# Rows of the score operands ordered by part, dimension and copy, in a fused decoder layer

## The chip, the cores and the metric

One core of a Trainium2 chip runs one launch of a whole decoder layer. The metric is the device time of that launch in microseconds, median of 3 runs.

## What is computed

```python
x = layernorm(x + attn(x, U))                         # 4 of its lines, R = 32
x = layernorm(x + xattn(ctx, ctx, x, Wq, ..., bo))    # cross-attention
x = layernorm(x + ffn(x, ...))                        # fake-quantised gate, up, down

# xattn: x is (1, 1024, 128), ctx is (1, 6404, 128), 16 heads of depth 8
qh = split_heads(q @ Wq + bq)
kh = split_heads(k @ Wk + bk)
vh = split_heads(v @ Wv + bv)
logits = einsum('bhsd,bhtd->bhst', qh, kh) / sqrt(8)
out = einsum('bhst,bhtd->bhsd', softmax(logits), vh)
return out @ Wo + bo
```

The cross-attention is nearly all of the work: 1024 queries against 6404 context rows in 16 heads.

## The kernel before

**Stages.** The first stretch, to about 118 us, does the first attention block and projects the context: for each of 17 chunks of 384 context rows (CK = 384, the last one partly filled) the keys are made in float32 and split into three bf16 parts, whose sum is the float32 key. They are written to an array in the chip's main memory, `k_parts_dram` [chunk, part, 128, CK]; the projected queries go the same way to `q_parts_dram` [half, part, 128, 512]. The middle stretch computes scores, exponentials and values. The last one, from about 820 us, projects the output, normalises and does the feed-forward block.

**Phases.** The middle stretch has 8 phases: 4 groups of 4 heads by 2 halves of 512 queries. Each phase goes over the 17 key chunks. For every chunk TensorE computes scores (line 1282: bf16, 59 rows contracted, 32 keys by 512 queries each) into PSUM, ScalarE turns most of them into exponentials (line 708, 128 x 1536 at a time, 67 instructions in a phase), VectorE computes the others with a polynomial (lines 958 to 984), and TensorE multiplies the result with the values (line 1312).

**The score operands.** A head has 8 dimensions (DH). A product of two float32 numbers is made of seven products of their bf16 parts, so that a head needs 7 x 8 = 56 contraction rows; three more rows carry a shift (59 = KR). `k_op` and `q_op` hold these rows on the partitions: two heads (i) lie side by side in a row, and the other two heads of the group (r, R2 = 2) lie 64 partitions on (W2 = 64). One row of `k_op` is 2 x 384 bf16 numbers, 1536 bytes; a row of `q_op` is 2048 bytes.

**The loads.** `load_k` (line 279) fills one of 4 slots (KS) of `k_op` for one chunk and group. It issues six DMAs at line 290: for each r one of 24 rows (key parts 0, 1, 2) and two of 16 rows (key parts 0 and 1, twice). `load_q` (line 295) fills one of 2 slots of `q_op` for one phase: for each r three DMAs at line 306, of 24, 16 and 16 rows, each of one query part read 3 or 2 times by a step of zero, and one of three rows for the shift (line 310). A slot has its own semaphore, and a DMA adds 16 to it: K_LOAD = 96 for a `load_k`, Q_LOAD = 128 for a `load_q`.

**Who issues them.** All these DMAs are issued by SyncE (SP in the profile, its queue SPq), one after the other in program order. In a phase it runs 12 `load_k` in a loop on the device (line 485, three turns of four; the address in main memory is worked out in registers by `sp.snap`), then one `load_k` for the last chunk, then `load_q` for the next phase, then four `load_k` for the next phase's first four chunks with fixed addresses, then, from the second phase on, four small DMAs of results at line 503 (`o_t<-att_rows`, 8 rows each). A `load_k` of slot s waits until TensorE has done the scores of the chunk that held s before (`scores_done`), four chunks back.

**Who waits for them.** TensorE waits for the next chunk's slot after the third block of scores of the present chunk, and for `q_loaded` at the start of a phase:

```python
if s == 2 and m + 1 < PHASES * NC:
    wait(k_loaded[(m + 1) % KS], at(K_LOAD * ((m + 1) // KS + 1), K_LOAD // KS))
```

Ahead of the first phase SyncE also issues the load for chunk 0 (line 420), the first `load_q` (448), the loads of chunks 1 to 3 (452), and only behind these the stores of the last four key chunks (454), for all of which it then waits before the loop of the first phase. A path for large scores (`general_shift_...`) calls the same two functions; it is not taken with these inputs.

Of the kernel before, what the change touches and what calls it, by code (L numbers as in the profile page):

```python
# [29 lines left out]
P = 128  # L30
# [4 lines left out]
HQ = 512  # L35
# [5 lines left out]
CK = CT * P  # L41
H = 16
DH = D // H
G = 4
NG = H // G
R2 = 2
G2 = G // R2
KR = 59
W2 = P // R2
# [40 lines left out]
def decoder_layer(nc, x, ctx_in, U, Wq, bq, Wk, bk, Wv, bv, Wo, bo, clip_x, clip_down,  # L90
                  w_gate, w_up, w_down, out, score_limit=SCORE_LIMIT):
    stack = ExitStack()
    with stack:
        def sb(name, shape, dt=F32):
            return stack.enter_context(nc.sbuf_tensor(name, shape, dt))
# [70 lines left out]
        k_op = sb("k_op", [P, KS, G2, CK], BF16)  # L166
        q_op = sb("q_op", [P, 2, G2, HQ], BF16)
# [111 lines left out]
        def load_k(sp, slot, chunk, group, signal, counter=None, count=None):  # L279


            src = k_parts_dram[chunk, 0, group, :]
            rows = P // (NG * R2)
            starts = [sp.snap(src.offset + r * (rows * CK)) for r in range(R2)]
            if counter is not None:

                sp.wait_ge(counter, count)
            for r in range(R2):
                for a, b, parts in ((0, 24, 3), (24, 40, 2), (40, 56, 2)):
                    sp.dma_start(k_op[W2 * r + a:W2 * r + b, slot, :, :].rearrange("p i t -> p (i t)"),  # L290
                                 bass.AP(src.tensor, starts[r],
                                         [[P * CK, parts], [G2 * CK, DH], [1, G2 * CK]])
                                 ).then_inc(signal, 16)

        def load_q(sp, slot, half, group_rows, group, signal, counter=None, count=None):

            src = q_parts_dram[half, 0, group_rows, :]
            rows = P // (NG * R2)
            starts = [[sp.snap(src.offset + n * (P * HQ) + r * (rows * HQ)) for r in range(R2)]
                      for n in range(3)]  # L300
            if counter is not None:

                sp.wait_ge(counter, count)
            for r in range(R2):
                for n, (a, b, copies) in enumerate(((0, 24, 3), (24, 40, 2), (40, 56, 2))):
                    sp.dma_start(q_op[W2 * r + a:W2 * r + b, slot, :, :].rearrange("p i t -> p (i t)"),  # L306
                                 bass.AP(src.tensor, starts[n][r],
                                         [[0, copies], [G2 * HQ, DH], [1, G2 * HQ]])
                                 ).then_inc(signal, 16)
                sp.dma_start(q_op[W2 * r + 56:W2 * r + 59, slot, :, :].rearrange("p i t -> p (i t)"),  # L310
                             shift_dram[half, group, :, G2 * r:G2 * r + G2, :].rearrange("j i t -> j (i t)")
                             ).then_inc(signal, 16)


        def general_shift_sp(sp):

            with sp.Fori(0, 2) as half:
                with sp.Fori(0, NG) as g:
                    n = half * NG + g
                    load_q(sp, 0, half, bass.ds(g * 32, 32), g, g_q_loaded, g_turned, n + 1)  # L320
                    with sp.Fori(0, NC) as c:
                        load_k(sp, 1, c, bass.ds(g * 32, 32), g_k_loaded,
                               g_scores_done, n * (NC * G) + c * G + 1)
                    dst = shift_dram[half, g, 0, :, :]
                    offsets = [sp.snap(dst.offset + j * (G * HQ)) for j in range(3)]
                    sp.wait_ge(g_shift_step, 5 * n + 5)
                    for j in range(3):
                        sp.dma_start(bass.AP(dst.tensor, offsets[j], [[P, 4], [HQ, G], [1, P]]),
                                     shift_parts[:, j, :]).then_inc(shift_written, 16)
# [51 lines left out]
        def _(sp):  # L381
# [36 lines left out]

            sp.wait_ge(k_parts_written[0], 16)
            load_k(sp, 0, 0, slice(0, 32), k_loaded[0])  # L420

            with sp.Fori(2, NC // 4) as r:
# [23 lines left out]
            sp.wait_ge(zero_shift_written, 16)  # L446
            sp.wait_ge(q_parts_written, 32)
            load_q(sp, 0, 0, slice(0, 32), 0, q_loaded[0])

            sp.wait_ge(scores_done, AHEAD)  # L450
            for c in range(1, KS):
                load_k(sp, c, c, slice(0, 32), k_loaded[c], k_parts_written[c], 16)
# [9 lines left out]
            with sp.If(sp.value_load(flag[0:1, 0:1]) > 0):  # L462
                all_written()
                sp.wait_ge(k_loaded[1], K_LOAD)
                general_shift_sp(sp)
                sp.wait_ge(shift_written, 48 * 2 * NG)

                load_q(sp, 0, 0, slice(0, 32), 0, g_q_loaded, g_turned, 2 * NG + 1)

                load_k(sp, 1, 1, slice(0, 32), g_k_loaded, g_scores_done, 2 * NG * NC * G + 1)  # L470
# [1041 lines left out]
```

## Time and profile before

| what | value |
|---|---|
| median of 3 runs | 873.7 us (872.42 to 881.33) |
| the profiled execution, its own time | 870.89 us |
| its span | 869.2 us |
| busy: PE, DVE, ACT, POOL | 719.9, 689.8, 738.2, 169.0 us |
| mean granted clock of TensorE | 0.953 of full speed |
| bytes read and written in main memory | 30.15 and 6.42 MB |

The span is what the profiler saw between the first and the last instruction; the execution's own time has 1.7 us more around it. PE is TensorE, DVE VectorE, ACT ScalarE, POOL GpSimd. SyncE computes nothing, so that the busy table of the page has no row for it; its DMA-issuing instructions stand in the views as SPq with a duration of their own, which is the time the issuing takes, not the transfer.

### The profile page before, as it was taken

The page shows a single profiled execution, that of the slowest core. Times are in us where ns is not written, and L with a number is a line of the kernel's source. Part 1 is how long each engine was busy: PE and PEld are TensorE (multiplying, and loading weights), DVE is VectorE, ACT ScalarE, POOL GpSimd, SP SyncE. Part 2 cuts the span into 40 slices and gives each one's busy share as a digit, 9 for nine tenths or more (in the row PEclk, how much of TensorE's full clock was granted, in tenths as well). Part 3 has the DMA queues.
Part 4 walks back from the last instruction along what each step waited for, and adds up shares of the span by engine and source line. Part 5 has one row for each costly group of instructions (what it writes and reads, how often), then busy time and mean ns, then how long its engine had stood idle before and what let it go on. Part 6 is the DMA issues. An engine that isn't in the chain of part 4 may idle for free.

```text
span 869.2 us, 38041 instructions
## 1 busy us (share of the span) xinstructions
PE 719.9 (83%) x15210; PEld 321.5 (37%) x15212; DVE 689.8 (79%) x1952; ACT 738.2 (85%) x650; POOL 169.0 (19%) x304
## 2 busy tenths in 40 slices
PE   6987678878899889879997899699878998899851
PEld 3435334423443344324433343233323443344331
DVE  3428749975999699939995999589958996899866
ACT  2446779997999999969997999799979997999842
POOL 2502412211222122202220222112211221122100
PEclk9999789998999999989999999999999999999965
DMA  3213321111111111111111111111111111111000
GB/s 104 77 55 115 126 82 35 33 42 40 36 34 40 40 36 36 40 39 37 35 38 41 36 35 36 44 36 35 35 44 37 35 35 44 37 34 35 23 1 25
DMA packets 31714, 38.38 MB, mean 44 GB/s; under 512 B 3534, under 2 KB 30192, under 8 KB 31616
## 3 DMA queue, kind: packets, MB, share of 16 engines
q1 hardware_dynamic: 30748, 36.57, 13.9%
q8 instruction: 65, 1.06, 0.5%
q10 hardware_dynamic: 868, 0.48, 0.2%
q14 instruction: 33, 0.27, 0.1%
HBM read 30.15 MB, written 6.42 MB: 42 GB/s over the span
## 4 chain that ended last, share of the span: by engine, by line
SPq 28%; ACT 25%; issue 18%; PE 17%; DMA 6%; DVE 5%; POOL 1%; ACTq 1%; POOLq 0%; DVEq 0%
SPq L290 24%; ACT probs L708 23%; PE ps L1312 7%; DMA k_op<-k_parts_dram 4%; PE ps L1282 3%; SPq L306 2%; PE ps L1211 2%; PE ps L1197 2%; SPq L503 1%; DMA k_parts_dram<-k_parts 1%; DVE stats L774 0%; POOL k_parts L539 0%; PE ps L1160 0%; DMA q_parts_dram<-q_parts 0%; DVE probs L1091 0%
## 5 line engine op out<-in xcount | busy, mean ns | idle before, releaser
L708 ACT ACTIVATE probs<-ps 128x1536 f32<-128x1536 f32 (+1 forms) x536 | 673.9, 1372 | 48.4 <-PE ps L1282 47.3
L1312 PE MATMUL ps<-probs,v_op 64*9 64x512 f32 (+1 forms) x8384 | 528.0, 503 | 48.2 <-DMA k_op<-k_parts_dram 42.2
L1282 PE MATMUL ps<-q_op,k_op 59*32 59x512 bf16 x6432 | 344.0, 386 | 52.0 <-ACT probs L708 42.5
L977 DVE SCALAR_TENSOR_TENSOR e_u<-e_u,e_f 128x256 f32<-128x256 f32 x720 | 259.6, 426 | 0.0
L1282 PEld LDWEIGHTS ps<-q_op,k_op 59*32 59x32 bf16 x6432 | 114.9, 91 | 318.7 <-issue 240.8
L1312 PEld LDWEIGHTS ps<-probs,v_op 64*9 64x9 f32 x8384 | 166.0, 87 | 139.0 <-issue 50.7
L958 DVE TENSOR_SCALAR e_t<-ps 128x256 f32<-128x256 f32 x240 | 90.7, 419 | 105.2 <-PE ps L1282 96.8
L586 POOL TENSOR_SCALAR e_pow<-e_t 128x512 int32<-128x512 int16 x120 | 74.3, 619 | 364.7 <-DVE e_t L958 364.7
L579 POOL COPY v_op<-v_all 128x108 f32<-128x108 f32 x136 | 62.6, 460 | 215.0 <-PE ps L1312 214.3
L977 DVE SCALAR_TENSOR_TENSOR e_u<-e_f 128x256 f32<-128x256 f32 x240 | 90.1, 417 | 0.2
L984 DVE SCALAR_TENSOR_TENSOR probs<-e_u,e_pow 128x256 f32<-128x256 f32 x240 | 89.6, 411 | 0.0
L964 DVE SCALAR_TENSOR_TENSOR e_f<-ps,e_t 128x256 f32<-128x256 f32 x240 | 89.4, 414 | 0.0
L539 POOL TENSOR_TENSOR k_parts<-probs,k_parts 128x384 bf16<-128x384 f32 x17 | 17.5, 1034 | 65.5 <-ACT k_parts L638 65.5
L665 ACT ACTIVATE probs<-ps,neg_n 128x1024 f32<-128x1024 f32 x8 | 8.9, 1115 | 16.8 <-PE ps L1211 16.8
L1160 PE MATMUL ps<-ctx_t,wk_turned 128*128 128x384 f32 x34 | 15.8, 547 | 6.4 <-ACT ctx_t L617 3.4
L625 ACT ACTIVATE kf<-ps,bias_cols 128x384 f32<-128x384 f32 x17 | 9.8, 579 | 8.8 <-PE ps L1160 8.8
L1163 PEld LDWEIGHTS ps<-wv_sb,ctx_t 128*128 128x128 f32 x102 | 14.8, 200 | 4.9 <-issue 0.6
L1211 PE MATMUL ps<-y_rhs,y_lhs 64*128 64x512 f32 x32 | 15.6, 611 | 0.7 <-DVE v_all L809 0.7
L1197 PE MATMUL ps<-probs,x_nat 128*128 128x512 f32 x32 | 15.6, 615 | 0.0
L638 ACT ACTIVATE k_parts<-probs 128x384 bf16<-128x384 f32 x17 | 8.8, 520 | 7.8 <-DVE probs L824 7.8
L809 DVE TENSOR_TENSOR v_all<-ps,bv_bc 128x384 f32<-128x384 f32 (+1 forms) x17 | 9.4, 556 | 7.5 <-PE ps L1163 7.4
L1163 PE MATMUL ps<-wv_sb,ctx_t 128*128 128x128 f32 x102 | 14.8, 283 | 0.0
(177 smaller groups left out, 247.1 us busy)
## 6 DMA issues: line engine op xcount, KB each, us to landing
k_op<-k_parts_dram SPq DMA_DIRECT2D x544, 24.0 KB
k_op<-k_parts_dram SPq DMA_DIRECT2D x272, 36.0 KB
k_parts_dram<-k_parts SPq DMA_DIRECT2D x17, 288.0 KB, 2.8
ctx_nat<-in_ctx_dram SPq DMA_DIRECT2D x16, 192.0 KB, 2.6
q_op<-q_parts_dram SPq DMA_DIRECT2D x32, 32.0 KB
q_parts_dram<-q_parts SPq DMA_DIRECT2D x2, 384.0 KB, 3.8
q_op<-q_parts_dram SPq DMA_DIRECT2D x16, 48.0 KB
x_nat<-in_x_dram SPq DMA_DIRECT2D x1, 512.0 KB, 3.7
```

The costliest lines, as they stand in the source:

```text
L290: sp.dma_start(k_op[W2 * r + a:W2 * r + b, slot, :, :].rearrange("p i t -> p (i t)"), bass.AP(src.tensor, starts[r], [[P * CK, parts], [G2 ...
L579: pool.tensor_copy(v_op[:, slot].rearrange("p j (h d) -> p j h d", h=G), v_all[:, bass.ds(tile, CT), head:head + G, :]).then_inc(v_staged, 1)
L586: pool.tensor_scalar(e_pow[:], e_low(e_t[:]), float(2 ** 23), float(EXP2_LEAD), ALU.mult, ALU.add).then_inc(e_pow_ready, 1)
L708: act.activation(probs[:, b % NP].rearrange("p u t -> p (u t)")[:, 0:columns], ps[:, bank:bank + BU, :].rearrange("p u t -> p (u t)")[:, 0 ...
L958: dve.tensor_scalar(e_t[:, cols], score, E_MIN, ROUND, ALU.max, ALU.add).then_inc(e_step, 1)
L964: dve.scalar_tensor_tensor(out=e_f[:, cols], in0=score, scalar=E_MIN, in1=e_low(e_t[:, cols]), op0=ALU.max, op1=ALU.subtract).then_inc(e_s ...
L977: dve.scalar_tensor_tensor(out=e_u[:, cols], in0=u[:, cols], scalar=a, in1=e_f[:, cols], op0=ALU.add, op1=ALU.mult).then_inc(e_step, 1)
L984: dve.scalar_tensor_tensor(out=probs[:, block % NP, BU - 1, 512 - EW + cols.start:512 - EW + cols.stop], in0=e_u[:, cols], scalar=EXP2[0], ...
L1197: last = pe.matmul(ps[:, 4 + b, :], x_nat[:, j, :], attn_e[:, j, HQ * b:HQ * b + HQ], start=(j == 0), stop=(j == TQ - 1), skip_group_check ...
L1211: last = pe.matmul(ps[:, 2 * (j % 2) + b, :], y_lhs[:, P * j:P * j + P], y_rhs[:, HQ * b:HQ * b + HQ], start=True, stop=True)
L1282: return pe.matmul(ps[a:a + P // G, bank, :], k_op[W2 * r:W2 * r + KR, kslot, i, P * j + a:P * j + a + P // G], q_op[W2 * r:W2 * r + KR, q ...
L1312: last = pe.matmul(ps[32 * k:32 * k + DH + 1, ACC[h], a:b], v_op[W2 * h:W2 * h + W2, slot, j, (DH + 1) * k:(DH + 1) * (k + 1)], probs[W2 * ...
```

## The change

Both operands keep seven blocks of 8 rows, and the seven pairs of parts are the same; their order changes. Before, a DMA's rows were ordered by part or copy first and dimension second (24, 16, 16 rows). Now they are grouped by the part of the key: rows 0 to 23 are key part 0 in three copies against the three query parts, rows 24 to 47 are key part 1 in the same way, rows 48 to 55 are key part 2 against query part 0. Within a DMA the dimension is the leading index, with 8 values, and the copy or part comes second. `load_k` now reads with a step of zero, and `load_q` reads several parts. The number of DMAs is the same (six and eight), as are the rows and bytes. `load_k` makes six start addresses where it made two; `load_q` makes two where it made six.

```diff
@@ load_k
-            starts = [sp.snap(src.offset + r * (rows * CK)) for r in range(R2)]
+            starts = [[sp.snap(src.offset + n * (P * CK) + r * (rows * CK)) for r in range(R2)]
+                      for n in range(3)]
...
             for r in range(R2):
-                for a, b, parts in ((0, 24, 3), (24, 40, 2), (40, 56, 2)):
-                    sp.dma_start(k_op[W2 * r + a:W2 * r + b, slot, :, :].rearrange("p i t -> p (i t)"),
-                                 bass.AP(src.tensor, starts[r],
-                                         [[P * CK, parts], [G2 * CK, DH], [1, G2 * CK]])
+                for part, (a, copies) in enumerate(((0, 3), (24, 3), (48, 1))):
+                    sp.dma_start(k_op[W2 * r + a:W2 * r + a + DH * copies, slot, :, :
+                                      ].rearrange("p i t -> p (i t)"),
+                                 bass.AP(src.tensor, starts[part][r],
+                                         [[G2 * CK, DH], [0, copies], [1, G2 * CK]])
                                  ).then_inc(signal, 16)
@@ load_q
-            starts = [[sp.snap(src.offset + n * (P * HQ) + r * (rows * HQ)) for r in range(R2)]
-                      for n in range(3)]
+            starts = [sp.snap(src.offset + r * (rows * HQ)) for r in range(R2)]
...
             for r in range(R2):
-                for n, (a, b, copies) in enumerate(((0, 24, 3), (24, 40, 2), (40, 56, 2))):
-                    sp.dma_start(q_op[W2 * r + a:W2 * r + b, slot, :, :].rearrange("p i t -> p (i t)"),
-                                 bass.AP(src.tensor, starts[n][r],
-                                         [[0, copies], [G2 * HQ, DH], [1, G2 * HQ]])
+                for a, parts in ((0, 3), (24, 3), (48, 1)):
+                    sp.dma_start(q_op[W2 * r + a:W2 * r + a + DH * parts, slot, :, :
+                                      ].rearrange("p i t -> p (i t)"),
+                                 bass.AP(src.tensor, starts[r],
+                                         [[G2 * HQ, DH], [P * HQ, parts], [1, G2 * HQ]])
                                  ).then_inc(signal, 16)
```

On SyncE, one `load_k` in the loop of the first phase was the following. ISA is the register instruction that works out an address; 24x1x768 and 16x1x768 are DMAs of 24 and 16 rows.

```order
L290 ISA
L290 DMA k_op<-k_parts_dram 24x1x768
L290 DMA k_op<-k_parts_dram 16x1x768 x2
L290 ISA
L290 DMA k_op<-k_parts_dram 24x1x768
L290 DMA k_op<-k_parts_dram 16x1x768 x2
```

The same `load_k` in the changed kernel (its line 291):

```order
L291 ISA
L291 DMA k_op<-k_parts_dram 24x1x768
L291 ISA
L291 DMA k_op<-k_parts_dram 24x1x768
L291 ISA
L291 DMA k_op<-k_parts_dram 8x768
L291 ISA
L291 DMA k_op<-k_parts_dram 24x1x768
L291 ISA
L291 DMA k_op<-k_parts_dram 24x1x768
L291 ISA
L291 DMA k_op<-k_parts_dram 8x768
```

Two DMAs of 24 rows and four of 16 became four of 24 and two of 8, and four more register instructions stand between them. Nothing else moved on SyncE in the loop.

Between two phases SyncE issues a `load_q` and four `load_k` with fixed addresses. Their start was:

```order
L306 DMA q_op<-q_parts_dram 24x1x1024
L306 DMA q_op<-q_parts_dram 16x1x1024 x2
L310 DMA q_op<-shift_dram 3x1024
L306 DMA q_op<-q_parts_dram 24x1x1024
L306 DMA q_op<-q_parts_dram 16x1x1024 x2
L310 DMA q_op<-shift_dram 3x1024
L290 DMA k_op<-k_parts_dram 24x1x768
L290 DMA k_op<-k_parts_dram 16x1x768 x2
```

and is now:

```order
L307 DMA q_op<-q_parts_dram 24x1x1024 x2
L307 DMA q_op<-q_parts_dram 8x1024
L312 DMA q_op<-shift_dram 3x1024
L307 DMA q_op<-q_parts_dram 24x1x1024 x2
L307 DMA q_op<-q_parts_dram 8x1024
L312 DMA q_op<-shift_dram 3x1024
L291 DMA k_op<-k_parts_dram 24x1x768 x2
L291 DMA k_op<-k_parts_dram 8x768
```

The sizes changed in the same way, with no register instructions in either.

## Rows read from the trace of the kernel before

**Rows 1.** Timeline, SyncE: start us, us, line, operation, count in a row.
```profile
383.70 2.70 SPq L503 DMA_DIRECT2D o_t<-att_rows  x4
386.80 64.30 SPq L290 DMA_DIRECT2D k_op<-k_parts_dram  x78
451.14 2.05 SPq L306 DMA_DIRECT2D q_op<-q_parts_dram  x3
453.23 0.44 SPq L310 DMA_DIRECT2D q_op<-shift_dram  x1
453.71 2.07 SPq L306 DMA_DIRECT2D q_op<-q_parts_dram  x3
455.82 0.44 SPq L310 DMA_DIRECT2D q_op<-shift_dram  x1
456.30 17.07 SPq L290 DMA_DIRECT2D k_op<-k_parts_dram  x24
```

**Rows 2.** Waits of SyncE, whole span: us in total, times, longest us.
```profile
SPq L290 <- PE ps L1282: 8.7, 16, 0.8
```

**Rows 3.** Timeline, ScalarE, around a change of phase.
```profile
429.25 32.49 ACT L708 ACTIVATE probs<-ps 128x1536 f32<-128x1536 f32 x26
465.13 1.45 ACT L708 ACTIVATE probs<-ps 128x1536 f32<-128x1536 f32 x1 [3.39 <-PE ps L1282]
```

**Rows 4.** Waits from 118 to 820 us.
```profile
ACT probs L708 <- PE ps L1282: 44.3, 25, 5.7
PE ps L1312 <- DMA k_op<-k_parts_dram: 42.2, 34, 4.9
```

**Rows 5.** Timeline around the last load.
```profile
810.41 11.60 ACT L708 ACTIVATE probs<-ps 128x1024 f32<-128x1024 f32 x9
810.47 2.04 SPq L290 DMA_DIRECT2D k_op<-k_parts_dram  x3
```

**Rows 6.** Line 290, whole span: duration ns min/median/max, first and last start us.
```profile
L290 SPq DMA_DIRECT2D k_op<-k_parts_dram x816: 611/658/834, 36.8 to 811.9; - x164
L290 SPq FUSED_REGOPS  x192: 42/47/80, 117.9 to 805.6; - x192
```

**Rows 7.** Line 290, single instructions: of 24 rows, of 16 rows, address.
```profile
L290 SPq DMA_DIRECT2D k_op<-k_parts_dram x1: 741/741/741, 424.3 to 424.3; - x1
L290 SPq DMA_DIRECT2D k_op<-k_parts_dram x1: 630/630/630, 425.9 to 425.9; - x1
L290 SPq MOVE k_op<-k_parts_dram x1: 38/38/38, 425.1 to 425.1; - x1
```

**Rows 8.** DMAs by size: count, KB each (page, part 6).
```profile
k_op<-k_parts_dram SPq DMA_DIRECT2D x544, 24.0 KB
k_op<-k_parts_dram SPq DMA_DIRECT2D x272, 36.0 KB
q_op<-q_parts_dram SPq DMA_DIRECT2D x32, 32.0 KB
q_op<-q_parts_dram SPq DMA_DIRECT2D x16, 48.0 KB
```

**Rows 9.** DMA packets and queues, from 376 to 465 us.
```profile
DMA packets 2336, 3.36 MB, mean 38 GB/s; under 512 B 288, under 2 KB 2176, under 8 KB 2326
q1 hardware_dynamic: 2326, 3.21, 12.1%
```

**Rows 10.** Other DMAs that SyncE issues: duration ns min/median/max.
```profile
L385 SPq DMA_DIRECT2D ctx_nat<-in_ctx_dram x16: 328/342/432, 1.3 to 83.8; - x16
L310 SPq DMA_DIRECT2D q_op<-shift_dram x16: 417/437/440, 95.1 to 727.1; - x16
L503 SPq DMA_DIRECT2D o_t<-att_rows x28: 624/637/687, 294.0 to 814.6; - x28
L435 SPq DMA_DIRECT2D ctx_nat<-in_ctx_dram x1: 662/662/662, 86.9 to 86.9; - x1
L414 SPq DMA_DIRECT2D shift_dram<-zeros_bf x1: 894/894/894, 35.9 to 35.9; - x1
```

**Rows 11.** Engines busy from 118 to 812 us, granted clock, DMA share.
```profile
118.00:812.00 694.00, 599.91 (x14302) 258.21 (x14291) 588.32 (x1680) 648.65 (x518) 132.94 (x248) 0.98 0.13 37
```

## The prediction

> **What bounds the kernel now.** The busy table offers ScalarE, so I began with the stretch of the eight phases: of 694 us ScalarE is busy 649, TensorE 600 at 0.98 of full clock, and the DMA engines only 0.13 [rows 11]. Bandwidth is free; ScalarE is near the bound, but not on it. The second view was what ScalarE waits for: 44.3 us in 25 waits for scores, and TensorE in turn 42.2 us for the key load [rows 4]. At a change of phase ScalarE runs without a pause and then stands 3.39 us [rows 3]. The third view says why the load is late: SyncE's timeline has no hole. 78 DMAs in 64.30 us, then 5.1 us of query DMAs, then 24 DMAs in 17.07 us [rows 1]. Its waits for freed slots, of which there could be over a hundred, come to 8.7 us in all [rows 2]. The turns of a phase add to 2.70 + 0.4 + 64.30 + 5.2 + 17.07 = 90 us, from 383.70 to 473.4. So what sets the length of a phase is the time that SyncE takes to issue, and ScalarE comes only 6 us behind (44.3 over seven changes of phase). The last `load_k` ends at 812.5, and the last exponentials at 822.0 [rows 5]: nine of them, about 1.3 us each, of which the last three belong to the last chunk. The last chunk's scores begin at about 817. A load lands 2 to 3 us after its issue (an estimate: the first of the 17.07 us run was issued by 460.6, and ScalarE goes on at 465.13 [rows 3], behind some 2 us of values and scores). So there are no more than 2 us to spare at the end.
>
> Hence a microsecond added to SyncE between 93 and 812 us costs one; one taken away gains one until about 44 are gone.
>
> **What the change does to that.** There are 136 `load_k` and 8 `load_q` [rows 8]; the first `load_k` lies in the setup, where it costs nothing. On SyncE's path that is 135 x 2 + 16 = 286 DMAs of 24 rows and 135 x 4 + 32 = 572 of 16 rows. A DMA of 24 rows takes 0.74 us to issue, one of 16 rows 0.63 to 0.66, I take 0.64 [rows 7]; the median of all is 0.658 [rows 6]. Before: 286 x 0.74 + 572 x 0.64 = 578 us. After: 572 of 24 rows at an unknown price, and 286 of 8 rows.
>
> The 8-row DMA has a near relative: line 503 moves 8 rows of 2048 bytes with the 8 leading, 0.637 us [rows 10]. 286 x 0.64 = 183 us. Below it could go to 0.44 (three rows, line 310), above to 0.69 (the longest of line 503): minus 57 to plus 15 us.
>
> The 24-row DMA whose leading count is 8 stands nowhere. First, what the leading count does. From 376 to 465 us SyncE issues 115 DMAs, and there are 288 packets under 512 bytes, though no row is that short [rows 9]: about 2.5 end marks for each DMA. Key loads led by 3, 2 and 2 would give 7 for three DMAs, 2.33 each, and the 8-row ones of line 503 more. A DMA thus runs on as many engines as its leading count lets it, and with 8 it runs on 8. Second, what issuing costs by that count: for rows without a second index 3 engines cost 0.437 and 8 cost 0.637 (lines 310 and 503), 0.04 for each engine more; 16 cost only 0.342 (line 385), so it isn't the number of rows (there 128). For rows with a second index 2 cost 0.63, 3 cost 0.74 [rows 7], 4 cost 0.662 (line 435, 128 rows), 8 cost 0.894 (line 414, 96 rows, a first issue behind a wait). From 2, 3 and 4 engines with 0.04 for each more one comes to 0.87, 0.94 and 0.82; line 414 says 0.89. I take 0.87. Lower end: 0.437, if what counts is rows per engine, which fall from 8 to 3; upper end: 1.27, if the step from 2 to 3 (0.107) goes on for six engines. 572 x 0.87 = 498 us. So the DMAs cost 498 + 183 - 578 = +103 us.
>
> The address instructions: `load_k` in the loop has 6 where it had 2. One takes 47 ns [rows 6]. To it comes a gap: of the 0.82 us per DMA in the loop (64.30 over 78) 0.66 are the DMA, 0.04 its MOVE [rows 7] and 0.02 its share of the old address instructions, which leaves 0.10 for some 2.3 gaps, 0.045 each. 96 loads x 4 x 0.09 = +35 us; from 18 (no gap) to 40. (SPq's 192 of them are these two for each of the 96 loads [rows 6].) Outside the loop addresses are fixed and nothing is added, and `load_q`'s four fewer don't exist at run time.
>
> The transfers get shorter: a DMA's engine moved 8 rows, now 3 or 1. A packet takes about 74 ns (12.1% of 16 x 89 us over 2326 packets) [rows 9], and an engine's are in series, so the last one lands some 0.4 us earlier. As SyncE sets the rate, that shifts the pipeline once: -0.4 us. TensorE's matmuls, 59 rows, are unchanged.
>
> Sum: +103 + 35 - 0.4, less up to 2 us spare at the end: +136. Against the profiled execution's own 870.9 us (2.8 below the median, near the fastest run): 1007 us. A loop load then takes SyncE 5.0 + 0.7 + 0.4 = 6.1 us, and ScalarE has work for 4.9 (32.49 us for 26, four to a chunk): it stands in every chunk, where it stood only at phase starts. That cover is what the kernel loses.
>
> Two rules of the Trainium skill bear on this. The trace has the end marks above. DMA: Bandwidth & Descriptors, Why a DMA increments its semaphore by 16 and not by 1, states that the engine count is the largest number up to 16 that divides both patterns' slowest dimension: 3, 2, 2 before and 8, 8, 8 now; the trace agrees in its 2.5 marks. The same page, Issuing engines are not separate DMA queues, calls the sequencer's time to initiate a DMA "usually small relative to the DMA itself". By that the change could only help. This trace disagrees: 0.66 us of issuing stands against 8 packets of 74 ns.
>
> **The rivals.**
> - **The price stays where 24 rows are now**, 0.74, whatever the leading count. For: the same 24 rows. Against: line 503 beside line 310. 572 x 0.74 = 423, + 183 - 578 = +28, with the addresses and less the 2 us +61: 932 us.
> - **All shapes with an 8 in front cost as line 503**, 0.64, since the second index costs nothing there. For: 4 engines with 128 rows cost 0.662. Against: line 414. 366 + 183 - 578 = -29, +35: 875 us, within 1%.
> - **Issuing gets cheaper with rows per engine.** At 0.55 for 24 rows and 0.5 for 8: 315 + 143 - 578 = -120, +35. SyncE then leaves the path and ScalarE takes it; the gain ends at its 44 us of waiting, from 827 to 860 us, say 845. Against: 16 and 24 rows both have 8 rows per engine and differ by 0.11; line 503 has one row per engine and costs 0.637.
> - **The landing decides, not the issuing**: TensorE waits for transfers on 2 or 3 engines, and 8 shorten each of the eight waits by 0.4 us: 868 us. For: rows 4 name the DMA. Against: no hole in rows 1, and the addresses would still count.
> - **Each engine costs 0.107 in these shapes**, so 1.27: +229 more, 1236 us. For: the step from 16 to 24 rows. Against: lines 435 and 414. TensorE falling to the lower clock as it waits more would also land above my range.
>
> **How the numbers follow.** A measurement of this kernel can tell about 1% from no change. Forecast 0.57 (973 to 1047 by prices of 0.81 to 0.94); price stays 0.17; as line 503 0.08; cheaper 0.07; landing 0.04; 1.27 or another slowdown above 0.07. Slower by over 1% takes the first, the second and the last, and a third of the line 503 case: 0.83. Within 1%: 0.08. Faster by over 1%: 0.09. The range: upward 1055, downward through the case at 932 and nearly to the one at 875, 880; what is left out is 0.07 above and some 0.15 below.
>
> **What would show it.** In the profile of the changed kernel: line 291's 24-row DMAs at 0.87 us and the 8-row ones at 0.64; 576 FUSED_REGOPS instead of 192; 8 end marks per DMA, so about 850 packets under 512 B per phase; SyncE without holes, phases of some 107 us; ScalarE waiting for scores 150 us or more, in over 100 waits; TensorE waiting for `k_op` in most chunks. Wrong would be: 24-row DMAs at or below 0.65, holes in SyncE's timeline, or a phase under 92 us.

## The result, and the profile after

The changed kernel takes 833.5 us, median of 4 runs, against 873.4 us before in the same comparison: ratio 0.955, 95% interval 0.948 to 0.961. It is faster by 40 us where I had forecast 136 us slower. The profiled execution took 833.0 us, its span 831.3.

The timeline of SyncE in the changed kernel, the counterpart of [rows 1]. The query loads are now line 307 and 312, the key loads line 291, the result copies line 505:

```profile
366.66 2.73 SPq L505 DMA_DIRECT2D o_t<-att_rows  x4
369.78 61.32 SPq L291 DMA_DIRECT2D k_op<-k_parts_dram  x78
431.14 1.91 SPq L307 DMA_DIRECT2D q_op<-q_parts_dram  x3
433.09 0.27 SPq L312 DMA_DIRECT2D q_op<-shift_dram  x1
433.41 1.91 SPq L307 DMA_DIRECT2D q_op<-q_parts_dram  x3
435.36 0.29 SPq L312 DMA_DIRECT2D q_op<-shift_dram  x1
435.69 15.56 SPq L291 DMA_DIRECT2D k_op<-k_parts_dram  x24
```

There is still no hole, but a round of this list, from 366.66 to 451.3, is 84.6 us where it was 90. Every piece that holds loads is shorter: 61.32 us for 64.30, 15.56 for 17.07 (16.7 to 16.9 in the other phases before). Line 312 is of special interest, since the change doesn't touch it: 0.27 and 0.29 us for 0.44.

Its waits: SyncE's (as [rows 2]), then from 118 to 820 us ScalarE's and TensorE's (as [rows 4]):

```profile
SPq L291 <- PE ps L1284: 8.4, 17, 0.7
...
ACT probs L710 <- PE ps L1284: 10.1, 17, 4.2
PE ps L1314 <- DMA k_op<-k_parts_dram: 9.1, 8, 4.0
```

ScalarE's timeline over the same change of phase as the first fence (as [rows 3]):

```profile
353.92 11.86 ACT L710 ACTIVATE probs<-ps 128x1536 f32<-128x1536 f32 x9
365.97 83.71 ACT L710 ACTIVATE probs<-ps 128x1536 f32<-128x1536 f32 x67 [0.20 <-PE ps L1284]
```

ScalarE does the 67 exponentials of a phase in 83.71 us without a pause. Its wait at the seven changes of phase was 1.4 to 5.7 us; here it is 0.2, and nowhere over 0.5. Of its 44.3 us of waiting 10.1 are left, 4.2 of them in one wait inside the first phase.

TensorE's clock tells the same story. Before, TensorE stood at a change of phase until a key load landed, and the clock granted to it then fell to its lower level, 1.2 GHz. The first row is TensorE's timeline before, the second the stretch that follows it, the third the changed kernel from 129 to 794 us (of the two stretches: start:end and length in us, the busy us of PE, PEld, DVE, ACT and POOL, then the granted clock):

```profile
463.10 1.16 PE L1312 MATMUL ps<-probs,v_op 64*9 64x512 f32 x16 [3.30 <-DMA k_op<-k_parts_dram]
463.96:467.37 3.41, 3.41 (x56) 2.09 (x48) 0.00 (x0) 1.52 (x2) 0.28 (x1) 0.50 0.13 41
129.00:794.00 665.00, 595.61 (x14443) 259.62 (x14429) 593.21 (x1696) 651.44 (x522) 139.13 (x248) 1.00 0.13 39
```

The trace of before shows such a fall at six of the seven changes of phase, for 3.4 or 6.8 us each; the changed kernel has none in that stretch. No run isolates what these falls cost. They come behind a late load, and the account of SyncE's time below needs nothing from them.

Line 291 over the whole span (as [rows 6]), and then single DMAs of it (as [rows 7]): 24 rows and 8 rows inside the loop, 24 rows and 8 rows among those with fixed addresses, and last the unchanged DMA of three rows, all 16 of them:

```profile
L291 SPq DMA_DIRECT2D k_op<-k_parts_dram x816: 278/685/1377, 36.9 to 771.7; - x164
L291 SPq FUSED_REGOPS  x576: 37/37/85, 117.2 to 767.5; - x192
...
L291 SPq DMA_DIRECT2D k_op<-k_parts_dram x1: 685/685/685, 402.1 to 402.1; - x1
L291 SPq DMA_DIRECT2D k_op<-k_parts_dram x1: 311/311/311, 403.0 to 403.0; - x1
L291 SPq DMA_DIRECT2D k_op<-k_parts_dram x1: 664/664/664, 448.1 to 448.1; - x1
L291 SPq DMA_DIRECT2D k_op<-k_parts_dram x1: 461/461/461, 448.8 to 448.8; - x1
L312 SPq DMA_DIRECT2D q_op<-shift_dram x16: 257/272/287, 95.6 to 691.7; - x16
```

The 576 address instructions are there as foreseen. The prices are not: 24 rows cost 0.66 to 0.70 us and not 0.87, 8 rows 0.31 or 0.46 and not 0.64.

Packets of one phase, 359 to 443 us, against [rows 9]:

```profile
DMA packets 2935, 3.35 MB, mean 40 GB/s; under 512 B 894, under 2 KB 2774, under 8 KB 2924
```

The small packets went from 288 to 894 in a phase, and 102 key DMAs with 8 end marks each make 816 of them. Read as the prediction reads them, one mark for each engine, each key DMA does run on 8 engines. That part of the change does what its shape says, and it isn't where the time came from, as the experiments show.

### The profile page after: what moved, and what is told of

It reads as the page before. It is cut to its first block, busy times and chain, and to the rows that moved or that the text cites. A ratio compares the mean times of both kernels' runs of the same rounds, so it can differ in the third digit from the quotient of the medians.

```text
span 831.3 us, 38425 instructions
## 1 busy us (share of the span) xinstructions
PE 707.7 (85%) x15210; PEld 319.9 (38%) x15212; DVE 689.5 (83%) x1952; ACT 736.0 (89%) x650; POOL 174.9 (21%) x304
## 4 chain that ended last, share of the span: by engine, by line
ACT 40%; issue 24%; PE 16%; SPq 10%; DVE 5%; DMA 3%; POOL 1%; ACTq 1%; POOLq 0%; DVEq 0%
ACT probs L710 39%; SPq L291 8%; PE ps L1314 6%; PE ps L1284 3%; PE ps L1213 2%; PE ps L1199 2%; DMA k_op<-k_parts_dram 2%; SPq L505 1%; DMA k_parts_dram<-k_parts 1%; PE ps L1162 1%; DVE stats L776 1%; PE ps L1449 1%; ACTq L723 1%; POOL k_parts L541 0%; DMA q_parts_dram<-q_parts 0%
## 5 line engine op out<-in xcount | busy, mean ns | idle before, releaser
L1284 PE MATMUL ps<-q_op,k_op 59*32 59x512 bf16 x6432 | 337.4, 382 | 60.7 <-ACT probs L710 56.4
L1284 PEld LDWEIGHTS ps<-q_op,k_op 59*32 59x32 bf16 x6432 | 107.9, 90 | 331.5 <-issue 245.7
L1314 PEld LDWEIGHTS ps<-probs,v_op 64*9 64x9 f32 x8384 | 169.3, 86 | 90.2 <-issue 27.7
L581 POOL COPY v_op<-v_all 128x108 f32<-128x108 f32 x136 | 68.3, 502 | 181.3 <-PE ps L1314 180.6
L1009 DVE STREAM_TRANSPOSE att_rows<-acc_t 128x512 f32<-128x512 f32 x7 | 5.0, 711 | 15.6 <-DMA o_t<-att_rows 15.6
L1165 PEld LDWEIGHTS ps<-wv_sb,ctx_t 128*128 128x128 f32 x102 | 15.5, 208 | 5.2 <-issue 1.2
```

Of the source, the lines that this page charges most:

```text
L581: pool.tensor_copy(v_op[:, slot].rearrange("p j (h d) -> p j h d", h=G), v_all[:, bass.ds(tile, CT), head:head + G, :]).then_inc(v_staged, 1)
L1284: return pe.matmul(ps[a:a + P // G, bank, :], k_op[W2 * r:W2 * r + KR, kslot, i, P * j + a:P * j + a + P // G], q_op[W2 * r:W2 * r + KR, q ...
L1314: last = pe.matmul(ps[32 * k:32 * k + DH + 1, ACC[h], a:b], v_op[W2 * h:W2 * h + W2, slot, j, (DH + 1) * k:(DH + 1) * (k + 1)], probs[W2 * ...
```

## The experiments

My theory after the result (A) was that the time of the eight phases is still SyncE's issuing time, one for one, and that I had the prices wrong. The rival (B) was that the 8 engines bring the rows in sooner, and the issuing follows from that.

### The dimension in front, and nothing else (lead_only)

```diff
-                                         [[P * CK, parts], [G2 * CK, DH], [1, G2 * CK]])
+                                         [[G2 * CK, DH], [P * CK, parts], [1, G2 * CK]])
...
-                                         [[0, copies], [G2 * HQ, DH], [1, G2 * HQ]])
+                                         [[G2 * HQ, DH], [0, copies], [1, G2 * HQ]])
```

> The kernel before with its row groups of 24, 16 and 16, its two addresses per load_k and its six DMAs; only the dimension (8) is put in front within each DMA. Theory A (issuing sets the time; what fell is mostly the price of the small DMA, which isn't here): 24 rows at 0.66 to 0.70 us, 16 rows at 0.60 to 0.64, a load_k cheaper by 0.1 to 0.3 us, 840 to 860 us. Theory B (the engine count is what matters, by landing or by issuing, and row sizes don't): 835 us or less, as after or better, since it has no added addresses.

Measured: 883.75 us, ratio to before 1.016 (1.013 to 1.019). It is slower by 1.6%, little but clear of the noise. The range of A was missed by 24 us, and B by 49: with 8 engines in every load the kernel is slower than with 2 and 3. Two DMAs of its loop, of 16 and of 24 rows:

```profile
L290 SPq DMA_DIRECT2D k_op<-k_parts_dram x1: 685/685/685, 410.5 to 410.5; - x1
L290 SPq DMA_DIRECT2D k_op<-k_parts_dram x1: 689/689/689, 411.4 to 411.4; - x1
```

24 rows became cheaper (0.74 to 0.69), but 16 rows dearer (0.63 to 0.66 before), and there are twice as many of them. That is what my range had wrong: I had put 16 rows led by 8 at 0.60 to 0.64.

### The new row groups, with the part or copy in front (sizes_only)

```diff
-                                         [[G2 * CK, DH], [0, copies], [1, G2 * CK]])
+                                         [[0, copies], [G2 * CK, DH], [1, G2 * CK]])
...
-                                         [[G2 * HQ, DH], [P * HQ, parts], [1, G2 * HQ]])
+                                         [[P * HQ, parts], [G2 * HQ, DH], [1, G2 * HQ]])
```

(against the changed kernel)

> The changed kernel with its row groups of 24, 24 and 8 and its six addresses, but the copy or part (3) put back in front of the dimension in the 24-row DMAs. Theory A: 24 rows at 0.72 to 0.74 us, 8 rows at 0.31 in the loop and 0.46 outside, together 0.1 to 0.2 us less per load_k than before: 845 to 860 us. Theory B: most of the load runs on 3 engines as before and the addresses cost, so 871 us or more.

Measured: 848.6 us, ratio 0.977 (0.972 to 0.983), as A expected. More than half of the gain is there with the 24-row DMAs still led by 3, and with the added addresses paid. It comes from the 8-row DMA that takes the place of a 16-row one: all of these together average 0.345 us, and the 16-row ones before averaged 0.640. A 24-row DMA in its loop:

```profile
L291 SPq DMA_DIRECT2D k_op<-k_parts_dram x1: 722/722/722, 412.6 to 412.6; - x1
```

### Four more addresses, or rather two (addresses)

```diff
-            starts = [sp.snap(src.offset + r * (rows * CK)) for r in range(R2)]
+            starts = [[sp.snap(src.offset + n * (P * CK) + r * (rows * CK)) for r in range(R2)]
+                      for n in (0, 1, 1)]
...
-                                 bass.AP(src.tensor, starts[r],
+                                 bass.AP(src.tensor, starts[n][r],
```

> The kernel before with six start addresses per load_k instead of two, DMAs of the same shapes (the two 16-row DMAs read key parts 1 and 2 in place of 0 and 1, so that part of each score product is another one; the work is the same). If the added register instructions cost what they last and their gaps (0.083 us each, 384 of them) on the queue that sets the time: 871 + 32 = 903 us. If they are hidden behind the issuing of the DMA before them: within 4 us of 871, with the durations of the DMAs shorter by what the registers take.

Measured: 888.8 us, ratio 1.020 (1.018 to 1.022). The compiled kernel merged the second and the third address, which are the same number, so that 192 were added and not the 384 that the expectation counts:

```profile
L291 SPq FUSED_REGOPS  x384: 37/37/85, 119.8 to 826.0; - x192
...
395.87 67.22 SPq L291 DMA_DIRECT2D k_op<-k_parts_dram  x78
```

17.3 us for 192 is 0.090 us each: nothing is hidden. It is the price that the prediction used. 78 DMAs with 24 added addresses take 67.22 us for 64.30 in [rows 1]. That pair differs by more than most; over the seven phases whose loop stands by itself in the timeline the mean went from 65.0 to 67.2 us, which is 0.090 for each address again. The DMAs' own durations are unchanged. (The kernel's result is another one, since it reads other parts; only its time is used.)

### The price of one shape by itself (probe)

SyncE issues four DMAs of one shape in a row, waits until they have landed, and goes on to the next, such as:

```diff
+            for i in range(4):
+                sem(sp.dma_start(dst[0:8, i, 0:384], a([[384, 8], [1, 384]])))
+            settle()
...
+            for i in range(4):
+                sem(sp.dma_start(dst[0:24, i, 0:384], a([[384, 8], [49152, 3], [1, 384]])))
+            settle()
```

> No decoder layer at all: SyncE alone issues four DMAs of one shape in a row, waits until all have landed, then the next shape; the output is zeros. Theory P1 (my prediction's: price grows with the engines, 0.04 us each, plus something for a second index): simple 3, 8 rows at 0.44, 0.64; 8x3 at 0.8 or more. Theory P2 (price grows with rows and index, not engines; a small DMA is short, and waits at its start for the rest of the one before it): simple 8 rows at 0.28 to 0.32 when the one before is small, 0.46 behind 8x3; 3 rows 0.27 behind 8 rows and 0.44 behind 2x8; 8x3 at 0.66 to 0.70. Source in SBUF: 0.62 if it is the source that makes line 503's dear, 0.3 if not.

Issue durations, ns min/median/max. In this order: simple 8 rows of 1536 bytes, 8 of 2048, 3 rows, 16 rows; then with a second index (the leading count first) 3x8, 2x8, 8x3, 8x2, 8x3 with a step of zero, 4x6, 16x3, 8x7; last 8 rows from SBUF:

```profile
L44 SPq DMA_DIRECT2D dst<-in_ctx_dram x4: 277/295/395, 2.2 to 3.3; - x4
L50 SPq DMA_DIRECT2D dst<-in_ctx_dram x4: 272/295/297, 7.3 to 8.3; - x4
L56 SPq DMA_DIRECT2D dst<-in_ctx_dram x4: 240/272/274, 12.3 to 13.2; - x4
L62 SPq DMA_DIRECT2D dst<-in_ctx_dram x4: 316/418/422, 17.0 to 18.3; - x4
L71 SPq DMA_DIRECT2D dst<-in_ctx_dram x4: 689/706/800, 28.8 to 31.1; - x4
L74 SPq DMA_DIRECT2D dst<-in_ctx_dram x4: 614/620/638, 33.9 to 35.9; - x4
L77 SPq DMA_DIRECT2D dst<-in_ctx_dram x4: 662/668/686, 38.5 to 40.6; - x4
L80 SPq DMA_DIRECT2D dst<-in_ctx_dram x4: 663/666/670, 42.8 to 45.0; - x4
L83 SPq DMA_DIRECT2D dst<-in_ctx_dram x4: 662/664/667, 47.2 to 49.3; - x4
L86 SPq DMA_DIRECT2D dst<-in_ctx_dram x4: 623/623/634, 51.5 to 53.5; - x4
L89 SPq DMA_DIRECT2D dst<-in_ctx_dram x4: 592/592/620, 55.9 to 57.8; - x4
L95 SPq DMA_DIRECT2D dst<-in_ctx_dram x4: 662/672/693, 65.6 to 67.8; - x4
...
L68 SPq DMA_DIRECT2D dst<-src_sb x4: 624/638/778, 24.6 to 26.8; - x4
```

A second index costs about as much as all the rest: 0.27 to 0.42 us for simple patterns, 0.59 to 0.71 with one. With 8 in front, rows and bytes don't matter in it: 16, 24 and 56 rows (8x2, 8x3, 8x7) have minima of 0.663, 0.662 and 0.662. Reading through a step of zero costs the same as reading apart. The rows also repeat what the loop showed: from 3x8 to 8x3 the 24 rows get cheaper, from 2x8 to 8x2 the 16 rows get dearer.

The same kernel then issues DMAs in mixed order. An 8-row one right behind two of 24 rows (8x3), a 3-row one behind 16 rows (2x8), a 3-row one behind 8 simple rows:

```profile
L105 SPq DMA_DIRECT2D dst<-in_ctx_dram x2: 461/464/467, 78.5 to 80.5; - x2
L109 SPq DMA_DIRECT2D dst<-in_ctx_dram x2: 426/428/429, 82.9 to 84.1; - x2
L117 SPq DMA_DIRECT2D dst<-in_ctx_dram x2: 272/272/273, 90.0 to 90.6; - x2
```

A small DMA right behind one with a second index takes some 0.16 us more than by itself. So part of such a DMA's cost is booked on its successor. That is the second half of P2: line 310's 0.437 in [rows 10] was 0.27 of its own and 0.16 of the 16-row DMA ahead of it. It also fits that an 8-row load costs 0.31 in the loop and 0.46 outside: in the loop an address instruction and a MOVE stand between, and they seem to take that time in its place. No run varies this alone.

### Rows from SBUF (probe_source)

The same, with other shapes, such as `sp.dma_start(dst[0:3, i, :], src_sb[32:35, :])`.

> SyncE's issuing by itself again, output zeros. My prediction took line 503 (8 rows, source in SBUF, 0.637) for the price of 8 rows from main memory. Theory S (the source in SBUF makes a DMA dear whatever its rows): 0.5 to 0.65 for 2, 3 and 8 rows from SBUF, against 0.25 to 0.30 from main memory. Theory E (engines make it dear, and only from SBUF): 0.3 for 2 rows, 0.62 for 8. 24, 48 and 56 rows of main memory in one index, which divide by 8 to 16: 0.30 to 0.43, so a second index costs 0.25 to 0.35.

From SBUF 2, 3, 8, 16 rows; from main memory 8, 24, 48 rows with one index (rows that lie one behind the other):

```profile
L44 SPq DMA_DIRECT2D dst<-src_sb x4: 569/574/734, 2.2 to 4.2; - x4
L47 SPq DMA_DIRECT2D dst<-src_sb x4: 640/643/687, 5.9 to 8.0; - x4
L50 SPq DMA_DIRECT2D dst<-src_sb x4: 624/634/672, 9.8 to 11.9; - x4
L53 SPq DMA_DIRECT2D dst<-src_sb x4: 554/586/589, 13.9 to 15.7; - x4
...
L65 SPq DMA_DIRECT2D dst<-in_ctx_dram x4: 288/296/343, 29.9 to 30.9; - x4
L74 SPq DMA_DIRECT2D dst<-in_ctx_dram x4: 297/365/366, 37.4 to 38.6; - x4
L80 SPq DMA_DIRECT2D dst<-in_ctx_dram x4: 320/418/423, 43.7 to 45.0; - x4
```

Theory S holds: a copy from SBUF to SBUF costs 0.57 to 0.64 us to issue, be it 2 rows or 16. Line 503, my relative for the 8-row load, was dear for its source and not for its 8 engines.

### The books of SyncE

Every DMA that SyncE issues from 93 us on, summed in each trace, plus 0.090 us for each address instruction more than before, beside the profiled executions' times:

| kernel | DMAs, us | against before | addresses added | sum | time against before |
|---|---|---|---|---|---|
| before | 605.2 | | | | 870.9 us |
| lead_only | 619.3 | +14.1 | 0 | +14.1 | +12.7 |
| sizes_only | 546.4 | -58.8 | 384 x 0.090 | -24.2 | -22.4 |
| changed kernel | 529.3 | -75.9 | 384 x 0.090 | -41.3 | -37.9 |

The sums come within 4 us of the measured times in all three, up and down. One query DMA of the kernel before, 0.77 us, starts just ahead of 93 us and is left out of its row; with it the last sum would be -42.1, 4.2 us from the measured time. From sizes_only to the changed kernel the 24-row DMAs go from 3 engines to 8; the issuing falls by 17.1 us and the time by 15.5. There is nothing left for an earlier landing.

### SyncE out of the way (seven_lead8, seven_lead7)

```diff
-                sp.dma_start(k_parts_dram[c0 + k].rearrange("a p t -> p a t"), k_parts[:, k % 4]
-                             ).then_inc(k_parts_written[k % 4], 16)
+                for at, first, last in ((0, 0, 2), (2, 0, 2), (4, 0, 3)):
+                    sp.dma_start(k_parts_dram[c0 + k, at:at + last, :, :].rearrange("a p t -> p a t"),
+                                 k_parts[:, k % 4, first:last]
+                                 ).then_inc(k_parts_written[k % 4], 16)
...
-                for a, b, parts in ((0, 24, 3), (24, 40, 2), (40, 56, 2)):
...
+                sp.dma_start(k_op[W2 * r:W2 * r + 7 * DH, slot, :, :].rearrange("p i t -> p (i t)"),
+                             bass.AP(src.tensor, starts[r], [[G2 * CK, DH], [P * CK, 7], [1, G2 * CK]])
+                             ).then_inc(signal, 16)
```

> The parts are stored seven times over in main memory in the order of the seven pairs (three stores per key chunk instead of one, four per half of the queries instead of one), so that a load_k is two DMAs of 56 rows, 8 dimensions in front, and a load_q four. By the probe a DMA of 8x7 takes 0.66 us to issue: a load_k takes SyncE some 1.7 us instead of 4.6. If issuing still sets the changed kernel's time, SyncE now waits for slots, ScalarE loses its last 10 us of waiting, and the loads of the setup get 6 us shorter: 812 to 828 us. If ScalarE or TensorE had already taken over (the gain of the change ended at the other engines), 830 to 836 us.

> As seven_lead8, but the seven parts stand in front of the 8 dimensions (7 x 8), so 7 engines and 0.73 us to issue. If with SyncE idle neither the price nor the engine count matters: within 3 us of seven_lead8. If landing matters: slower by more.

Measured: 830.2 and 829.8 us, ratios 0.950 (0.949 to 0.952) and 0.950 (0.948 to 0.951). By the bounds that I had set, 830.2 is the second case (the others had taken over); the first case, 812 to 828 us, was missed. The trace shows that both cases hold in part. Of seven_lead8, SyncE's wait for slots in the whole span, and ScalarE's for scores from 118 to 780 us:

```profile
SPq L289 <- PE ps L1283: 371.3, 129, 3.7
...
ACT probs L709 <- PE ps L1283: 1.4, 7, 0.2
```

SyncE waits 371 us for slots, and ScalarE waits 1.4 us instead of 10. The phases got faster: from phase to phase the first exponential comes 84.0 us later each time (84.5 after the first phase), against 83.9 to 85.6 in the changed kernel after its first. But the setup got longer: eight query stores take SyncE 5.9 us where two took 1.1, the key stores are tripled, the first `load_q` is issued at 102.6 us and not at 93.6, and the first exponential starts at 109.1 us and not at 101.1. The two nearly cancel. Seven parts or eight dimensions in front make no difference once SyncE has time.

### The sevenfold store for the keys alone (seven_keys, after_again; seven_keys_five, after_five)

```diff
-                for n, at, copies in ((0, 0, 2), (1, 2, 2), (2, 4, 2), (0, 6, 1)):
...
+                sp.dma_start(q_parts_dram[half].rearrange("a p t -> p a t"), q_parts[:, half]
+                             ).then_inc(q_parts_written, 16)
```

(against seven_lead7; the key blocks are then in the order 0, 1, 2, 0, 1, 0, 1, and `load_q` is that of the kernel before)

> As seven_lead7, with the sevenfold store for the keys alone; the queries are stored and loaded as in the kernel before (two stores, eight DMAs per load_q). In the phases SyncE still has time to spare, so phases of 84.0 us as there; in the setup six query stores (some 0.65 us each) go and some 2 us of query loads come: 826 to 830 us, 1 to 3 us under seven_lead7. Theory that the phases' bound is still SyncE: slower than seven_lead7 by the 0.3 us per phase of added load_q.

> The changed kernel once more, on the same chip as seven_keys, so that the two can be compared: 833 us.

Measured on one chip: 830.2 us (828.7 to 831.3) and, for the changed kernel once more, 834.5 (831.6 to 834.7). The 1 to 3 us under seven_lead7 that I expected did not show, though that kernel ran on another chip. ScalarE's timeline in seven_keys, two phases:

```profile
282.31 83.81 ACT L708 ACTIVATE probs<-ps 128x1536 f32<-128x1536 f32 x67 [0.20 <-PE ps L1282]
366.31 83.71 ACT L708 ACTIVATE probs<-ps 128x1536 f32<-128x1536 f32 x67 [0.20 <-PE ps L1282]
```

The ranges lay 0.3 us apart, so both ran again with more rounds:

> seven_keys once more with more rounds, beside the changed kernel on the same chip. If its phases of 84.0 us (ScalarE without a pause) gain more than its setup loses (first exponentials at 107 instead of 102 us): 2 to 5 us under the changed kernel, about 829.

> The changed kernel with more rounds, for that comparison: 832 to 835 us.

Measured: 828.8 us (828.4 to 830.0) against 834.3 (834.1 to 837.3). Now 4 us lie between the ranges. This version beats the changed kernel by 5.5 us. In these two traces its first exponential comes 6.3 us later (108.7 us against 102.4), and from there to the last one it takes 10.4 us less (672.4 for 682.8): what it gains is the rest of ScalarE's waiting.

## Why the prediction was wrong

**What bounds the kernel: right.** The step from the timeline without holes to "a microsecond on SyncE costs one" held in three kernels, within about 4 us each. So did the limit on the other side: seven_lead8 shows that with SyncE waiting for slots ScalarE's work of 84.0 us per phase is the bound. The changed kernel stands right at it: after its first phase three phases last 83.9 to 84.0 us, ScalarE's own pace, and the next three 84.6 to 85.6, where SyncE is again a little slower. Its phases are thus under the 92 us that the prediction had named as a sign of being wrong.

**Address instructions: right in their price, with a rebate that I had not seen.** +35 us was forecast for 384; at the measured 0.090 each they cost 35 of SyncE's time. But 192 of them stand right ahead of an 8-row DMA. These DMAs average 0.316 us in the loop and 0.462 outside, 28 us less for the 192, so that about as much as those addresses and the MOVEs beside them take came back there (an estimate; no run takes these addresses away).

**The engine count, right, and its role, wrong.** The loads run on 8 engines. But "what issuing costs by that count, 0.04 for each engine more" was read from lines 310 and 503, and these two differ in more than engines. Line 310's 0.437 held 0.16 of the DMA ahead of it; line 503's 0.637 is the price of a source in SBUF. By themselves and from main memory 3 rows cost 0.272 and 8 rows 0.295: the slope was not 0.04 but 0.005. Line 414, which seemed to confirm it with 0.894, reads SBUF too. One of my own rows spoke against the slope: line 385, which I put at 16 engines, costs 0.342, less than line 310 with 3. I used it against the number of rows only.

**The 8-row DMA: the first term that failed.** 286 x 0.64 = 183 us was forecast. They took 104 (0.363 on average, about 0.31 in the loop and 0.46 outside). My lower end of 0.44 was above it: it rested on line 310 and was too high by that row's 0.16.

**The 24-row DMA: the second.** 572 x 0.87 = 498 us was forecast, 400 measured (0.700). The term had the wrong sign and not only the wrong size: from 3 in front to 8, with all else alike, a 24-row key load in the phases went from 0.739 us on average in sizes_only to 0.701 in the changed kernel. The price was below the 0.74 of before, which I had held for the second most likely case. 79 and 98 us, with 3 of the three-row DMAs, make up the difference between the +103 forecast for the DMAs and the -75.9 of the books. The time fell into what the rival "gets cheaper" allowed, 827 to 860 us, but not for its reason, rows per engine, nor at its prices of 0.55 and 0.5 us: in lead_only the 16-row DMAs went from 8 rows per engine to 2 and became dearer, from 0.640 to 0.685 on average.

**The landing: not it.** With 8 engines in every load lead_only was slower, and the books leave nothing for it. That seven or eight in front gave the same time agrees, but two counts so close to each other are a weak test of it.

**The rule that I set aside.** The Trainium skill (DMA: Bandwidth & Descriptors, Issuing engines are not separate DMA queues) calls initiating a DMA "usually small relative to the DMA itself". Here 0.66 us of issuing stood against 0.6 us of an engine's transfer (8 packets of 74 ns), and in three kernels the time followed the issuing, so that it was not small in what it did. The same page's rule on the engine count (Why a DMA increments its semaphore by 16 and not by 1) agrees with the 894 marks. What failed was neither rule but the relatives that I took prices from, without asking what else set them apart.

## What to carry to other kernels

Where one queue issues many small DMAs, look for holes in its timeline first: without any, the shapes are to be priced by what they take to issue. Here 16, 24 or 56 rows in two indices with 8 in front were bought at one price. Look for a form with one index, a source in main memory, and few DMAs, and count each address that is worked out in a loop. A row that serves as the price of another must agree with it in source, in number of indices and in what stands ahead of it on the queue; where no row does, a kernel of nothing but DMAs settles it in one run.

## What the runs showed of the hardware that I had not expected

- A second index costs more than the rows: 16 rows took 0.418 us to issue in one index and 0.620 in two (2x8), 24 rows 0.365 in one and 0.668 in two (8x3), by the medians of four.
- In two indices with 8 in front the number of rows didn't count (8x3 and 8x7: 0.662 each, at the least). The price differed with the leading count, but not in order: 16x3 0.592, 2x8 0.614, 4x6 0.623, 8x3 0.662, 3x8 0.689, again at the least.
- SBUF to SBUF took 0.57 to 0.64 us to issue for 2, 3, 8 and 16 rows; from main memory it was 0.25, 0.27, 0.30 and 0.42.
- A DMA with two indices lengthened a small one right behind it by 0.16 us. Behind another small one, three rows took 0.272. With two register instructions between them, as in the loop of the changed kernel, 8 rows took 0.31 us and not 0.46.
- TensorE's granted clock fell to 0.50 of full speed for 3.4 us after it had stood 3.3 us for a late load.
- What makes these prices was not looked into; they are what the rows show for these shapes.
